# Loads issued six chunks ahead instead of seven, all eight slots filled at the start, one half load in narrow pieces

## The reference

```python
x = x + conv(_gn(x), w_up, b_up, w_left, b_left, w_right, b_right)
# in conv:
xp = jnp.pad(x, ((0, 0), (0, 0), (1, 1), (1, 1)))
xp = xp.at[:, :, DST_R, DST_C].set(xp[:, :, SRC_R, SRC_C])
up = _conv(xp, w_up * jnp.asarray(_UP), b_up)      # stride (2, 2)
out = out.at[:, :, 0::2, 0::2].set(up)             # left at 1::2, 0::2, right at 1::2, 1::2
return out * jnp.asarray(OUT_MASK)
```

## Time and profile before

| | |
|---|---|
| median of three runs | 741.6 us |
| the profiled execution | 742.11 us |
| its span | 740.3 us |
| engines busy: PE, DVE, ACT, POOL | 655.8, 613.8, 574.8, 473.9 us |
| DMA packets | 267034, 269.62 MB |
| loads of 1 MiB, issue to landing | 126, median 11.1 us |
| stores of 1 MiB, issue to landing | 128, median 11.1 us |

### The profile page before, as it was taken

How to read it: one execution, slowest core, us unless ns; L and a number is a source line. 1 busy time by engine, 2 the same in 40 slices (tenths; PEclk the granted TensorE clock), 3 DMA queues, 4 the chain that set the end, 5 groups by cost and what they waited for, 6 DMA issues and landing times.

```text
span 740.3 us, 36046 instructions
## 1 busy us (share of the span) xinstructions
PE 655.8 (89%) x15484; PEld 602.8 (81%) x15484; DVE 613.8 (83%) x1793; ACT 574.8 (78%) x1235; POOL 473.9 (64%) x1109
## 2 busy tenths in 40 slices
PE   1699999999999989889889898898898988989893
PEld 1589999999999888778788787787887878878883
DVE  4999999999999778788787787887977878878740
ACT  3488888988888787787877877878778778787782
POOL 1177777787776765756657657566576575665774
PEclk9989999999999999999999999999999999999997
DMA  8999999999999999999999999999999999999998
GB/s 262 349 362 384 384 380 373 367 367 374 374 356 366 366 367 370 365 379 368 366 369 367 374 370 367 374 365 362 379 361 375 362 366 376 365 365 374 378 352 286
DMA packets 267034, 269.62 MB, mean 364 GB/s; under 512 B 4656, under 2 KB 266800, under 8 KB 266992
## 3 DMA queue, kind: packets, MB, share of 16 engines
q1 hardware_dynamic: 266512, 269.24, 106.0%
q10 hardware_dynamic: 480, 0.00, 0.0%
HBM read 135.01 MB, written 134.22 MB: 364 GB/s over the span
## 4 chain that ended last, share of the span: by engine, by line
DMA 36%; DVE 31%; ACT 12%; POOL 10%; SPq 4%; issue 3%; PE 3%; POOLq 0%; ACTq 0%
DMA xs<-in_x 35%; DVE stats L229 17%; ACT tn L313 12%; DVE tn L277 7%; POOL xs L401 5%; POOL tn L411 4%; SPq L193 3%; PE bank L459 3%; DVE small L261 2%; DMA out<-xs 1%; DVE nmr L272 1%; DVE small L265 1%; DVE rstd L268 1%; DVE var L250 1%; DVE mate L237 0%
## 5 line engine op out<-in xcount | busy, mean ns | idle before, releaser
L459 PE MATMUL bank<-tn,wts 64*64 64x192 f32 (+1 forms) x15360 | 646.9, 325 | 0.0
L459 PEld LDWEIGHTS bank<-tn,wts 64*64 64x64 f32 x15360 | 593.4, 137 | 34.1
L229 DVE BATCH_NORM_STATS2 stats<-xs 128x6 f32<-128x512 f32 x512 | 350.4, 697 | 95.1 <-DMA xs<-in_x 95.1
L401 POOL TENSOR_TENSOR xs<-res,xs 128x192 f32<-128x192 f32 (+6 forms) x775 | 376.1, 530 | 7.7 <-ACT res L336 5.8
L313 ACT ACTIVATE tn<-xs,nmr,rstd 128x256 f32<-128x256 f32 x511 | 258.9, 592 | 78.7 <-DVE nmr L272 78.1
L336 ACT ACTIVATE res<-bank,bias 64x512 f32<-64x512 f32 (+5 forms) x640 | 302.1, 472 | 21.1 <-PE bank L459 10.9
L411 POOL COPY tn<-tn 128x128 f32<-128x128 f32 (+2 forms) x320 | 97.3, 362 | 242.2 <-ACT tn L313 242.2
L277 DVE TENSOR_SCALAR tn<-xs,rstd,nmr 128x256 f32<-128x256 f32 x513 | 181.5, 427 | 2.3
L470 PEld LDWEIGHTS bank<-blank 128*128 128x128 f16 x64 | 6.1, 96 | 82.5 <-ACT res L336 65.8
L470 PE MATMUL bank<-blank 128*128 128x2 f16 x64 | 11.2, 176 | 63.9 <-POOL tn L411 63.8
L307 ACT ACTIVATE std<-var 128x16 f32<-128x16 f32 x64 | 13.8, 216 | 49.7 <-DVE var L250 49.7
(11 more groups left out here) (18 smaller groups left out, 24.1 us busy)
## 6 DMA issues: line engine op xcount, KB each, us to landing
out<-xs SPq DMA_DIRECT2D x128, 1024.0 KB, 11.1
xs<-in_x SPq DMA_DIRECT2D x126, 1024.0 KB, 11.1
xs<-in_x SPq DMA_DIRECT2D x4, 512.0 KB, 8.4
tn<-in_L_conv_w_up SPq DMA_DIRECT2D x1, 256.0 KB, 3.8
tn<-in_L_conv_w_left SPq DMA_DIRECT2D x1, 256.0 KB, 4.3
tn<-in_L_conv_w_right SPq DMA_DIRECT2D x1, 256.0 KB, 6.2
bias<-in_L_conv_b_up ACTq DMA_DIRECT2D x2, 0.2 KB, 4.5
bias<-in_L_conv_b_left ACTq DMA_DIRECT2D x2, 0.2 KB, 6.0
```

The source lines that it names most:

```text
L229: last = nc.vector.bn_stats(stats[:, k % 2, 2 * u:2 * u + 2].rearrange("p g a -> p (g a)"), both)
L401: last = nc.gpsimd.tensor_tensor(onto, frm, onto, ALU.add)
L459: last = nc.tensor.matmul(psum[bank + j][to:to + C, at:at + cols], wts[first:first + C, NT * rect[0] + n, :], taps(b, rect, tap, first), s ...
```

## The change

AHEAD becomes 6, and the loads before the loop now fill all eight slots, chunks 1 to 7. In the loop, loads are issued from chunk 8 on: that of chunk k + 6 beside the store of chunk k, for k from 2 to 57. It waits for the stores of chunk k - 2. The load of chunk 7's first half (LATE) is issued as sixteen transfers of eight partitions each, all on a semaphore of their own, narrow_loaded. A transfer of eight partitions uses eight of the transfer engines, one of 128 partitions all sixteen. DVE waits for all sixteen of them; later loads into that slot and half count one less on their own semaphore. No other engine's program is changed.

```diff
--- before.py
+++ after.py
@@ -63,7 +63,9 @@
 
 QUARTER = G // 4
 HALF = (slice(0, G // 2), slice(G // 2, G))
-AHEAD = 7
+AHEAD = 6
+LATE = (SLOTS - 1, 0)
+NARROW = 8
 
 
 WRAPS = [
@@ -132,6 +134,7 @@
             return tn[1][W_AT[t][0]:W_AT[t][0] + C, at:at + C]
 
         loaded = [[sem(f"loaded{s}_{half}") for s in range(SLOTS)] for half in range(2)]
+        narrow_loaded = sem("narrow_loaded")
         stored = [sem(f"stored{s}") for s in range(SLOTS)]
         w_loaded = [sem(f"w_loaded{t}") for t in range(3)]
         b_loaded = sem("b_loaded")
@@ -186,7 +189,11 @@
 
             def load(k, half):
                 frm, to = part(x_dram, k, HALF[half])
-                sp.dma_start(to, frm).then_inc(loaded[half][k % SLOTS], 16)
+                if (k, half) == LATE:
+                    for p in range(0, P, NARROW):
+                        sp.dma_start(to[p:p + NARROW], frm[p:p + NARROW]).then_inc(narrow_loaded, 16)
+                else:
+                    sp.dma_start(to, frm).then_inc(loaded[half][k % SLOTS], 16)
 
             def store(k, half):
                 to, frm = part(out_dram, k, HALF[half])
@@ -197,7 +204,7 @@
             for n in range(4):
                 frm, to = part(x_dram, 0, slice(QUARTER * n, QUARTER * (n + 1)))
                 sp.dma_start(to, frm).then_inc((quarter[n // 2], loaded[n // 2][0])[n % 2], 16)
-            for k in range(1, AHEAD):
+            for k in range(1, SLOTS):
                 for half in range(2):
                     load(k, half)
 
@@ -206,24 +213,31 @@
                 for half in range(2):
                     sp.wait_ge(bank_added, NB * (k + 1) if k < NCHUNK - 1 else NB * k + 4 + 2 * half)
                     store(k, half)
-                    if n < NCHUNK:
-                        if n >= SLOTS:
-                            sp.wait_ge(stored[n % SLOTS], 32 * (n // SLOTS))
+                    if SLOTS <= n < NCHUNK:
+                        sp.wait_ge(stored[n % SLOTS], 32 * (n // SLOTS))
                         load(n, half)
             for s in range(SLOTS):
                 sp.wait_ge(stored[s], 32 * (NCHUNK // SLOTS))
 
         @block.vector
         def _(dve):
+            def wait_half(k, half):
+
+                if (k, half) == LATE:
+                    dve.wait_ge(narrow_loaded, 16 * (P // NARROW))
+                else:
+                    earlier = k // SLOTS - ((k % SLOTS, half) == LATE)
+                    dve.wait_ge(loaded[half][k % SLOTS], 16 * (earlier + 1))
+
             def bn(k, u0, u1):
 
                 if k >= NCHUNK:
                     return
                 s = k % SLOTS
                 if k and u0 in (0, G // 4):
-                    dve.wait_ge(loaded[4 * u0 // G][s], 16 * (k // SLOTS + 1))
+                    wait_half(k, 4 * u0 // G)
                 if k and u0 == 0 and u1 == G // 2:
-                    dve.wait_ge(loaded[1][s], 16 * (k // SLOTS + 1))
+                    wait_half(k, 1)
                 for u in range(u0, u1):
                     both = view(xs, (s * G + 2 * u) * PIX, [(1, PIX), (PIX, 2)])
                     last = nc.vector.bn_stats(stats[:, k % 2, 2 * u:2 * u + 2].rearrange("p g a -> p (g a)"), both)
```

## The result

The changed kernel takes 753.8 us (median of four runs, 753.36 to 754.11) against 741.6 us: the ratio is 1.0167, with a 95% interval of 1.0153 to 1.018. That is 12.2 us slower, and outside the range that was given (737.0 to 749.0 us). The profiled execution has a span of 751.6 us, 11.3 more than before.

What follows compares the result with a forecast made beforehand. Transfers were taken as the bound, with one trailing engine of sixteen setting a beat of 11.4 us a chunk. The sum 5.7 + 0.5 - 2.3 - 2.4 = +1.5 on 741.6 gave 743.1 us, range 737.0 to 749.0.

Steps and rivals of the forecast that it cites:

- (a): Queue order: two more stores pass through the trailing engine ahead of the last load's landing, +5.7 us.
- (b): Start: chunk 7's halves join the pure loads, four stores run with no load between; +0.5 us.
- (d): Loads into a slot no longer wait for stores: 16 chunks at 0.15 us gained, -2.4 us.
- second rival: Waits had slowed the trailing engine all along; removing them gives -7.8 us, total 737.7 us; chance 0.27.
- (c): Chunk 7's narrow half spares the trailing engine 3.0 us, less 0.7 idle: -2.3 us; other end +3.0.
- first rival: The trailing engine is among the eight carrying the narrow half: +3.0 us there, total 748.4 us; chance 0.23.
- third rival: The narrow half relieves nobody, spared engines stand idle: 0 to +0.7 us, total 745.4 to 746.1 us; chance 0.1.
- theory A: After the result: two more stores cost 6 us, removed wait nothing, narrow half idles spared engines, trailing one included, 6 us.

Runs made afterwards that it cites:

- e1: The changed kernel with chunk 7's first half loaded as one transfer of 128 partitions: 747.66 us, ratio 1.0082.
- e9: e1 up to chunk 46, where two chunks' loads are issued beside one chunk's stores; from then on seven ahead with the waits: 742.0 us, ratio 1.0009.
- e5: e1 with the last chunk's load issued one round earlier, beside that of chunk 62: 749.87 us.
- e2: The kernel before, seven ahead with its waits, with chunk 6's first half in sixteen transfers of eight partitions: 747.89 us, ratio 1.0076.
- e13: The kernel before plus 0.5 MB of unread loads behind the first loads, eight transfers of eight partitions four apart: 743.45 us, ratio 1.0031.
- e15: As e13, but each added transfer over eight neighbouring partitions: 748.72 us, ratio 1.0102.
- e11: As e10, but partitions 0 to 63 in eight transfers of seven partitions and two of four: 752.48 us.
- e3: The changed kernel with its sixteen narrow transfers spread, one or two behind each of the first loads: 758.68 us.
- e8: e3 with each narrow transfer over partitions four apart: 752.08 us.
- e10: Six ahead, chunk 7's first half spread behind first loads: partitions 0 to 63 in eight transfers four apart, 64 to 127 in one: 752.95 us.
- e7: The changed kernel with each of the sixteen narrow transfers over partitions four apart: 755.86 us.

## Why the prediction was wrong

The frame held: transfers bound the kernel, one engine sets their beat, and 41.4 us follow the last load's landing (41.6 measured). The forecast was +1.5 us, the change brings +12.2. Step by step:

**(a) and (b), order and start: right.** They were put at 5.7 + 0.5 = 6.2 us; e1, which has them and the removed wait, measures 6.0, and e9, which puts the order right before the tail, takes nearly all of it back. The 0.5 of (b) alone is within e9's error. What the step did not say is that the last loads count as a row, and not the last alone (e5).

**(d), the wait: mis-sized, -2.4 for nothing.** I took the difference between the first beats (11.25 us) and the later ones (11.40) as the cost of the leading engines' running dry. But in the changed kernel, where SP waits for no store, the beat rises in the same way, from 10.87 to 11.14 to 11.38 us, and e9's 46 chunks without the wait gain nothing. So the rise is not the price of the wait; why the first beats are shorter is not shown. The lead of the other engines did not grow either, against the 9 us that the step expected. Here are three stores from the traces, as us behind the first engine, the first two from the middle of the kernel before and of the changed one, the third from the end of the kernel before:

```
413.11  0.00 0.06 0.12 0.15 0.40 0.50 0.58 0.59 0.90 0.96 2.41 2.48 2.51 2.70 3.19 3.75
412.52  0.00 0.32 0.33 0.37 0.38 0.40 0.40 0.52 0.63 0.64 0.70 0.85 1.01 2.56 2.75 3.96
730.78  0.00 0.01 0.03 0.04 0.10 0.13 0.14 0.15 0.24 0.26 0.27 0.81 1.49 1.62 1.69 2.93
```

From 200 to 680 us the last engine is 3.6 us (median) behind the first in the kernel before, and 3.9 in the changed one. The third row also corrects a reading: the last engine trails twelve others by over 2 us, but three by only 1.2 to 1.4. The share of 0.28 from 731 to 732 us, four engines' worth, had said so. The lower bound of the step, "its rate is its own", was the value. The second rival, that the waits had slowed the trailing engine, has fallen with it.

**(c), the narrow half: the wrong sign, and a term that was missing.** It was put at -2.3 us, with +3.0 as the other end. Measured: +6.1 (the change against e1) and +6.2 (e2). Two pieces of it are shown. The trailing engine is among the eight that carry the half, so the extra 64 packets lengthen the run: 2.0 us in e13, at most 3.2. That was the first rival, priced at 3.0; nothing in the rows before had named the half, and I put the likelier story on the wrong one. The rest, 3 to 4 us, was in no step: I priced every packet of the narrow transfers at the rate of wide ones. Engines that write neighbouring partitions slow each other, and others that come by: 5.3 us for eight transfers, by e15 against e13. In the changed kernel this shows from 54 to 58 us, where full engines move 229 GB/s: (348 - 229) / 348 x 4 = 1.4 us. From 58 to 60 us (315 GB/s) it is 0.2 more, and from 48 to 52 us, where 284 and 270 GB/s go through per unit of share instead of 316, 0.5. That makes 2.1, an estimate from these windows; with the 2.0 of e13, how the remaining 2 us fall is not shown. Windows under 340 GB/s were to show idle engines; those from 54 to 58 us had none idle. And the landing that was to show the wrong eight engines, 706 us, was passed: 710.04. The first rival's whole sum was 748.4 us, still 5.4 short of the 753.8 measured: it lacks the same term, and has the -2.4 of (d). So the range was too narrow: its upper end added the bounds of the terms that I had, and none for a form of transfer that the trace of before doesn't contain.

The idle engines, which the third rival had and which theory A took for the cause after the result, are real (share 0.55 to 0.61 from 50 to 54 us). By e13 they are not the ones that set the beat, so I hold their idle time for free; no run isolates it.

By the Trainium skill ("DMA: Bandwidth & Descriptors", latency and other measured facts) engine 7 is one of the two that are usually slower, which fits a trailing engine among the lowest eight and not among the lowest two. Whether it is number 7, no run here shows; e11 was to tell, and its own slow transfer hid it.

## What to carry to other kernels

When transfers bound a kernel and one transfer engine trails, the time is that engine's work up to the last load plus what follows the landing: count the transfers queued in front of the last loads, and don't pay for a deeper queue, which here brought nothing (e9). Leave transfers at all 128 partitions; a narrow one over neighbouring partitions is not merely uneven, it slows packets on all engines while it is worked off (e2, e15). To learn on which side of such a split a slow engine is, add a dummy load to one side and look whether the total moves.

## What the runs showed of the hardware that I had not expected

The order of partitions sets the speed of a transfer. Eight neighbours cost 5.3 us more than eight partitions four apart (e15, e13), for eight transfers of 64 KB; sixteen of them, spread, hold all engines at 276 GB/s where 338 are reached four apart (from 14 to 36 us, e3 and e8); and the stretch with a transfer of partitions 64 to 127 runs at 195 GB/s with all engines busy (e10). The Trainium skill ("SBUF — State Buffer", Door 1, the DMA port swizzle) has the rule: four neighbouring partitions, and those 32 above them, share one of sixteen ports, and 64 partitions reach only eight ports, for which it gives 196 GB/s. The runs agree with it in kind. That e10's stretch comes to nearly the same number is not a test of it, since two thirds of its bytes are of other transfers. Wide transfers alone, in the usual order, ran at 348 GB/s.

A step between partitions makes an issue dearer: 677 ns against 284 at the least (e7, the changed kernel), enough to empty a queue that had 9 us of work.

The rate depends on the mix: 348 GB/s while only loads run, 384 once loads and stores alternate and before the beat has risen (81 to 104 us: 385 and 381 in the kernel before, 383 and 384 in the changed one, 385 in e1).
